# Transformer block in fp32 on one core: the attention's value products taken two chunk steps at a time

## The chip, the cores and the metric

One core of a Trainium2 chip runs the whole kernel. The metric is the device time of one execution in microseconds; lower is better. Its engines are TensorE (PE; PEld is its weight loading), VectorE (DVE), ScalarE (ACT), GpSimd (POOL) and SyncE (SP), which issues the transfers.

## The reference

For 32 sequences of 512 rows and 256 features, in fp32: `x = x + attention(layernorm(x))`, then `x = x + 0.5 * ffn(layernorm(x))`.

The attention is linear: 16 heads of 16 features, `phi(x) = elu(x) + 1` of the projected queries and keys, in 4 chunks of 128 rows, with a state S and a running sum of keys z carried from chunk to chunk:

```python
scores = jnp.where(mask, jnp.einsum('bqd,bkd->bqk', qi, ki), 0)
num = jnp.einsum('bqk,bkd->bqd', scores, vi) + jnp.einsum('bqd,bde->bqe', qi, S)
den = jnp.sum(qi * (jnp.cumsum(ki, axis=1) + z[:, None, :]), axis=-1, keepdims=True)
out = num / den
S2 = S + jnp.einsum('bkd,bke->bde', ki, vi)
```

The result goes through Wo. The FFN has 1024 hidden features, weights in integers with a scale per group of 128 rows, and SiLU between its two products.

## The kernel before, in words

A pass of the loop works on three sequences at once: the attention of sequence i, the FFN of sequence i - 1, and layer norm, projections and features (phi) of sequence i + 1. Each engine has its own instruction list, written out by hand in a function: `pe_iteration`, `ve_iteration`, `ac_iteration`, `po_iteration`, `sp_iteration`. An engine works its list in order; `w.need(event, shift, k)` puts a wait for an event of this or a neighbouring pass in front of the next instruction. Flags A, Fn, N say which of the three parts a pass has. Pass 0 has no FFN, passes 1 to 30 have all, pass 31 has no next sequence, pass 32 only an FFN.

The attention has U = 8 steps: u = 4 t + c, for two halves t of the heads and four chunks c. For a step:
- `scores(u)` (L442): four matmuls into two PSUM banks `sc[0]` and `sc[1]`. It waits until the scores of the step before have left these banks.
- The causal mask: `mask_half` (L601) on VectorE multiplies a bank by `causal` into the tile `probs[u % 2]`. For the steps in `POOL_MASKS` = 2, 3, 4, 5 the second half goes another way: `copy_scores` (L943) on ScalarE copies `sc[1]` to `probs`, GpSimd multiplies it in place (L1005).
- `update_state(u)` (L464) adds the chunk to the state, `snapshot(u)` (L709) on VectorE copies it out, `from_state(u)` (L452) multiplies the queries by it.
- `values(u)` (L480): the masked scores times the values, into `num[t]`, on tiles of 32 columns of the array; sixteen matmul records, of which four run side by side.
- The reciprocals of the denominators: transposed by `spread_reciprocals` (L512) into a bank and copied out by `reciprocals_out` (L936), once for each t. `attention(t)` (L722) multiplies them in.

Between the steps stands the FFN, for slices j = 0 to 7 of the hidden features: `fc1(j)` (L379, L380) writes two banks, a and b. `ffn_scaled(j)` (L850, ScalarE) takes bank a, `ffn_sum(j)` (L687, VectorE) adds bank b, `ffn_silu(j)` (L858, L861, ScalarE) applies SiLU and makes the high part s_hi, and GpSimd the low part s_lo (L998). Behind the steps come the next sequence's `x_transposes` (L347), whose two banks ScalarE copies to xt_hi (L839) and VectorE to xt_lo (L631), then `project_kq(0)` and `project_kq(1)` (L317, twelve matmuls each), and the second FFN product `fc2` and the output projection (also L317).

PSUM has eight banks: num[0], num[1], state_acc, sc[0], sc[1], and a ring of three. `RING` gives each use of a ring bank its number, in order of time; a use waits for the last reader of the use before it in the same bank (`free_bank`). `BORROWED` puts some uses into the other banks.

On TensorE the middle of a pass reads: scores(0), k transposes, fc1(0), fc1(1), update(0), fc1(2), scores(1), update(1), values(0); then for u = 2 to 7: fc1(u + 1), reciprocals at u = 2 and 4, scores(u), update(u), from_state(u - 1), values(u - 1), with x_transposes at u = 6 behind them. project_kq(0), from_state(7), values(7), project_kq(1) follow. On ScalarE, for j = 3 to 6: scale slice j, reciprocals out at 3 and 5, copy the scores of step j - 1, SiLU of slice j - 1; then slice 7 scaled, xt_hi, and SiLU of 6 and 7.

Of the kernel before, what the change touches and what calls it, by code (L numbers as in the profile page):

```python
# [29 lines left out]
P = 128  # L30
# [43 lines left out]
def build(nc, x, wq_t, bq, wk_t, bk, wv_t, bv, wo_t, bo, gamma, beta, q1, sc1, b1, q2, sc2, b2, out):  # L74
# [4 lines left out]
    C = S // P  # L79
# [15 lines left out]
    with ExitStack() as ctx:  # L95
# [66 lines left out]
        def by_group(ap):  # L162
# [11 lines left out]
        RING = {"ht0": 0, "v1": 2, "kt1": 1, "f1a": 0, "f1b": 2, "f2a": 1, "f2b": 0, "f3a": 2, "f3b": 1, "rb0": 0,  # L174
                "f4a": 2, "f4b": 1, "f5a": 0, "f5b": 2, "rb1": 1, "f6a": 0, "f6b": 2, "f7a": 1, "f7b": 0,
                "xt0": 2, "xt1": 1, "k0": 0, "q0": 1, "z0": 0, "wo0": 2, "z1": 1}
        USES = list(RING)
        NEXT_USES = {"xt0", "xt1", "k0", "q0"}

        BORROWED = {"v0": state_acc, "kt0": state_acc, "ht1": num[0], "f0a": num[0], "f0b": num[1], "wo1": num[0]}  # L180
# [51 lines left out]
        def need_masked(w, u, r):  # L232
# [29 lines left out]


        LAST_READ = {
            "ht0": (ht_l, 0), "v1": (v_sb, 3), "kt1": (kt_sb, 1), "rb0": (rb_sb, 0),
            "rb1": (rb_sb, 1), "z0": (e_out, 0), "z1": (e_out, 1), "wo0": (e_x1, 0),
            "xt0": (xt_l, 0), "xt1": (xt_l, 1), "k0": (phi, 0), "q0": (phi, 1),
        } | {f"f{j}{ab}": ((f_a, f_b)["ab".index(ab)], j) for j in range(FT) for ab in "ab"}

# [4 lines left out]
        def free_bank(w, use, present):  # L274

            if use == "v0":
                w.need(snap, -1)
                return
            if use == "kt0":
                w.need(v_sb, 0, 1)  # L280
                return
            if use == "ht1":
                w.need(e_x1, -1, 1)
                return
            if use == "f0a":
                w.need(ht_l, -1, 1)
                return
            if use == "f0b":
                if "rb0" in present:
# [60 lines left out]
        def pe_iteration(e, i, A, Fn, N, N2, preparation=None, bias_products=None, first=False):  # L350
# [95 lines left out]
            def from_state(u):  # L446

                t, c = divmod(u, C)
                if c:
                    n = t * (C - 1) + c - 1  # L450
                    w.need(snap, 0, n)
                    e.matmul(num[t][:, c * P:(c + 1) * P], state[:, n % 3, :], phi_q[:, t, c * P:(c + 1) * P],  # L452
                             start=False, stop=False, skip_group_check=True)

            def update_state(u):
                t, c = divmod(u, C)
# [11 lines left out]
            def values(u):  # L468

                t, c = divmod(u, C)  # L470
                for r in range(2):
                    need_masked(w, u, r)
                w.need(v_sb, 0, c)
                if c == 0 and Fn:
                    w.need(f_b, -1, 0)
                if u == C:
                    w.need(rden, 0)
                for odd in range(2):
                    for pair in range(HT // 2):
                        last = e.matmul(  # L480
                            num[t][32 * pair:32 * pair + 32, c * P:(c + 1) * P],
                            v_pad[:, c, t * HT // 2 + pair, 2 * odd:2 * odd + 2, :],
                            probs[u % 2][:, 2 * pair + odd, :],
                            start=(c == 0 and odd == 0), stop=(odd == 1), skip_group_check=True)
                av_pe.done(last)

            def denominators(shift):
# [12 lines left out]
            def denominators_back(shift):  # L500

                w.need(den_sb, shift)
                for x in range(2):
                    last = e.transpose(num[1][:, (2 + x) * P:(3 + x) * P], den_rows[:, x * P:(x + 1) * P], ident[:, :])
                den_tr.done(last)

            def spread_reciprocals(t):

# [29 lines left out]
                k_transposes(0)  # L538
                k_transposes(1)
            fc1(0)  # L540
            fc1(1)
            if not A and Fn:
                fc1(2)
                for j in range(FT):
                    if j + 3 < FT:
                        fc1(j + 3)
                    fc2_group(j)
                return
            if A:
                update_state(0)  # L550
            fc1(2)
            if A:
                scores(1)
                update_state(1)
                values(0)
            for u in range(2, U):
                if u < 7:
                    fc1(u + 1)
                if A and u in (2, 4):
                    spread_reciprocals(u // 2 - 1)  # L560
                if A:
                    scores(u)
                    update_state(u)
                    from_state(u - 1)
                    values(u - 1)
                if u == 6 and N:
                    x_transposes()
            if preparation:
                preparation()
            project_kq(0)  # L570
            if A:
                from_state(U - 1)
                values(U - 1)
            project_kq(1)
            if bias_products:
                bias_products()
# [12 lines left out]


        def half_probs(u, r):
            return probs[u % 2][:, r * HV:(r + 1) * HV, :]

        def mask_half(e, w, u, r):

            w.need(sc_pe, 0, u)
            if u >= 2:
                w.need(av_pe, 0, u - 2)
            else:
                w.need(av_pe, -1)  # L600
            masked[r].done(e.tensor_tensor(  # L601
# [31 lines left out]
        def ve_iteration(e, i, A, Fn, N, N2, preparation=(None, None, None)):  # L633
# [121 lines left out]
            if Fn and not A:  # L755
                ffn_scaled(0)
            ffn_sum(0)
            ffn_sum(1)
            if A:
                snapshot(0)  # L760
            ffn_sum(2)
            if A:
                mask(1)
                snapshot(1)
            for u in range(2, U):
                if u < 7:
                    ffn_sum(u + 1)
                if A:
                    mask(u)
                    snapshot(u)  # L770
# [4 lines left out]
                if N and u == 6:  # L775
                    for t in range(T):
                        ve_lo(e, w, ring_bank(f"xt{t}")[:, :], xt_hi, xt_lo, t, xt_h, 1, xt_l)
# [56 lines left out]
        def ac_iteration(e, i, A, Fn, N, N2, preparation=None):  # L834
# [81 lines left out]
            if A:  # L916
# [5 lines left out]
                for n in range(2):  # L922
# [4 lines left out]
            ffn_scaled(0)  # L927
            ffn_scaled(1)
            ffn_silu(0)
            ffn_scaled(2)  # L930
            ffn_silu(1)

            def reciprocals_out(t):
                if A:
                    w.need(rb_pe, 0, t)
# [2 lines left out]
            def copy_scores(u):  # L938

                if A and u in POOL_MASKS:  # L940
                    w.need(sc_pe, 0, u)
                    w.need(av_pe, 0, u - 2)
                    copied.done(e.activation(half_probs(u, 1), sc[1][:, :].rearrange("p (h q) -> p h q", h=HV), ACT.Copy))  # L943

            for j in range(3, FT - 1):
                ffn_scaled(j)
                if j in (3, 5):
                    reciprocals_out((j - 3) // 2)
                copy_scores(j - 1)
                ffn_silu(j - 1)  # L950
            copy_scores(FT - 2)
            ffn_scaled(FT - 1)
            if N:
                for t in range(T):
                    w.need(v_pe, 0)
# [349 lines left out]
```

How the kernel before makes its waits and increments, by code:

```python
    def need(self, event, shift=0, k=None):  # L63
        k = event.per - 1 if k is None else k
        if self.known.get((id(event), shift), -1) >= k:
            return
        self.known[(id(event), shift)] = k
        value = event.value(self.i + shift, k)
        if not isinstance(value, int) or value > 0:
            self.engine.wait_ge(event.sem, value)
# [1034 lines left out]
        @block.sync  # L1106
        def _(e):
            e.dma_start(x_in[:, :, :], x_v[0]).then_inc(load.sem, 16)
            src = {"q": wq_t, "k": wk_t, "v": wv_t, "o": wo_t}
            for n in WORDER:
                e.dma_start(stage_of(n), src[n].rearrange("(t p) n -> p t n", p=P)).then_inc(p_wdma[n], 16)
            e.dma_start(bias_o[:, :], on_all(bo)).then_inc(p_dma, 16)
            for t in range(T):
                e.dma_start(w1_i[t], q1[t * P:(t + 1) * P, :]).then_inc(p_wdma["1"], 16)
            early(e, store)
            e.wait_ge(p_const, CONSTS - 1)
            e.wait_ge(p_zero, 1)
            sp_iteration(e, -1, False, False, True, True, lambda: e.wait_ge(p_v, V_W1))
            for n in range(2):
# [10 lines left out]
            with e.Fori(1, B - 2) as i:  # L1131
                sp_iteration(e, i, True, True, True, True)
            sp_iteration(e, B - 2, True, True, True, False)
            sp_iteration(e, B - 1, True, True, False, False)
            sp_iteration(e, B, False, True, False, False)
            e.wait_ge(store.sem, store.value(B - 1, 1))
```

## Time and profile before

| | |
|---|---|
| time, median of 3 runs | 1603.43 us (1603.17 to 1604.33) |
| the profiled execution | 1604.64 us, span 1602.9 us |
| mean granted TensorE clock | 0.990 |
| PE busy | 1556.0 us, 97% |
| DVE busy | 1238.6 us, 77% |
| ACT busy | 1177.6 us, 73% |
| POOL busy | 827.3 us, 52% |

The profile is of one execution. Times inside it count from the first instruction. Busy time of PE is modelled at the ends of matmuls: a row's duration reaches over the start of the next, and the distance between two starts tells how long TensorE was held.

### The profile page before, as it was taken

What the parts mean: (1) busy time and instruction counts of PE and PEld (TensorE: products, weight loads), DVE (VectorE), ACT (ScalarE), POOL (GpSimd) and SP (SyncE); (2) the same over time, 40 slices, a digit from 0 to 9 for tenths busy, and PEclk for the clock granted to TensorE, in tenths of its full rate; (3) what the DMA queues carried; (4) which work ended last, traced back from release to release, by engine and by line L of the source; (5) the groups of instructions that cost most, each with busy time, mean ns of one, the idle gap of its engine ahead of it and who ended that gap; (6) DMA issues with size and microseconds to landing.
All of it is one profiled execution on the core that took longest, in us unless ns stands there. A gap on an engine that the chain in (4) does not pass through costs nothing.

```text
span 1602.9 us, 39179 instructions
## 1 busy us (share of the span) xinstructions
PE 1556.0 (97%) x13668; PEld 1346.5 (84%) x13668; DVE 1238.6 (77%) x2587; ACT 1177.6 (73%) x2045; POOL 827.3 (52%) x594
## 2 busy tenths in 40 slices
PE   5799999999999999999999999999999999999997
PEld 4588888888888888888888888888888888888886
DVE  6777787777787777787778787778787778787865
ACT  4487777787777787777797777787777787777763
POOL 3255445555445555445555445555445555445553
PEclk8799999999999999999999999999999999999999
DMA  7756675545664546764456664446765546764440
GB/s 187 172 125 141 170 159 127 128 123 143 170 164 118 121 134 144 170 168 120 115 132 147 170 154 133 113 130 151 170 145 130 126 124 155 170 158 116 114 99 27
DMA packets 153943, 222.94 MB, mean 139 GB/s; under 512 B 20032, under 2 KB 71488, under 8 KB 153920
## 3 DMA queue, kind: packets, MB, share of 16 engines
q1 hardware_dynamic: 152560, 222.63, 57.5%
q8 instruction: 14, 0.23, 0.1%
q10 hardware_dynamic: 1360, 0.01, 0.0%
q14 instruction: 9, 0.07, 0.0%
HBM read 138.69 MB, written 83.89 MB: 139 GB/s over the span
## 4 chain that ended last, share of the span: by engine, by line
PE 64%; DVE 15%; ACT 9%; issue 9%; DMA 2%; DVEq 1%; SPq 1%; ACTq 0%; POOL 0%
PE ring L317 31%; DVE probs L601 7%; PE sc L317 6%; PE num L480 5%; PE sc L442 4%; PE ring L379 4%; ACT silu_f L850 3%; PE ring L380 3%; PE num L317 3%; PE state_acc L317 3%; ACT silu_f L858 2%; DVE x_hat L623 2%; DVE silu_f L687 2%; PE num L452 2%; DVE xt_lo L631 1%
## 5 line engine op out<-in xcount | busy, mean ns | idle before, releaser
L998 POOL TENSOR_TENSOR s_lo<-silu_f,s_hi 128x512 fp32r<-128x512 f32 x256 | 341.6, 1339 | 357.5 <-ACT s_hi L861 357.4
L687 DVE SCALAR_TENSOR_TENSOR silu_f<-ring,scale,silu_f 128x512 f32<-128x512 f32 x222 | 166.4, 749 | 177.1 <-ACT silu_f L850 176.1
L317 PE MATMUL ring<-w_hi,s_hi 128*128 128x256 f32 x992 | 282.0, 284 | 1.4 <-issue 1.4
L317 PE MATMUL ring<-w_lo,s_hi 128*128 128x256 f32 x992 | 278.9, 281 | 0.0
L317 PE MATMUL ring<-w_hi,s_lo 128*128 128x256 f32 x992 | 278.8, 281 | 0.0
L601 DVE TENSOR_TENSOR probs<-sc,causal 128x512 f32<-128x512 f32 x384 | 251.0, 681 | 12.2 <-PE sc L442 8.8
L1018 POOL TENSOR_TENSOR qk<-qk,phi_q 128x512 f32<-128x512 f32 x64 | 82.8, 1294 | 264.0 <-DVE qk L654 264.0
L442 PE MATMUL sc<-q_stack,k_stack 96*128 96x256 f32 x1024 | 189.0, 300 | 11.7 <-issue 4.8
L317 PEld LDWEIGHTS ring<-w_hi,s_hi 128*128 128x128 f32 x992 | 187.2, 189 | 15.5 <-issue 14.0
L1005 POOL TENSOR_TENSOR probs<-probs,causal 128x512 f32<-128x512 f32 x128 | 165.2, 1291 | 56.9 <-ACT probs L943 51.5
L379 PE MATMUL ring<-gt_hi,w_q 128*128 128x512 f32 x441 | 193.7, 439 | 0.0
L317 PEld LDWEIGHTS ring<-w_lo,s_hi 128*128 128x128 f32 x992 | 187.1, 189 | 1.2
L317 PEld LDWEIGHTS ring<-w_hi,s_lo 128*128 128x128 f32 x992 | 187.4, 189 | 0.0
L442 PEld LDWEIGHTS sc<-q_stack,k_stack 96*128 96x128 f32 x1024 | 153.3, 191 | 37.7 <-DVE probs L601 14.5
L380 PE MATMUL ring<-gt_lo,w_q 128*128 128x512 f32 x441 | 174.3, 395 | 0.0
L858 ACT ACTIVATE silu_f<-silu_f 128x512 f32<-128x512 f32 x256 | 159.8, 624 | 14.7 <-DVE silu_f L687 10.9
L982 ACT ACTIVATE state<-num 128x256 f32<-128x256 f32 x32 | 12.3, 384 | 215.2 <-PE num L495 215.2
L861 ACT ACTIVATE s_hi<-silu_f 128x512 fp32r<-128x512 f32 x256 | 162.0, 633 | 8.1
L850 ACT ACTIVATE silu_f<-ring,bias,scale 128x512 f32<-128x512 f32 x217 | 166.2, 766 | 0.5
L480 PE MATMUL num<-probs,v_pad 128*32 128x128 f32 x4096 | 166.0, 280 | 0.5 <-DVE probs L601 0.3
L480 PEld LDWEIGHTS num<-probs,v_pad 128*32 128x32 f32 x4096 | 96.9, 110 | 31.8 <-issue 1.1
L379 PEld LDWEIGHTS ring<-gt_hi,w_q 128*128 128x128 f32 x441 | 83.0, 188 | 44.9 <-issue 30.7
(188 smaller groups left out, 3972.0 us busy)
## 6 DMA issues: line engine op xcount, KB each, us to landing
k_stack<-k_rows SPq DMA_DIRECT2D x192, 256.0 KB, 4.1
q_stack<-q_rows SPq DMA_DIRECT2D x384, 128.0 KB, 6.1
k_rows<-silu_f SPq DMA_DIRECT2D x128, 256.0 KB, 3.6
q_rows<-probs SPq DMA_DIRECT2D x128, 256.0 KB, 4.7
x_in<-in_x SPq DMA_DIRECT2D x32, 512.0 KB, 8.1
xb<-in_x SPq DMA_DIRECT2D x32, 512.0 KB, 7.8
out<-clip SPq DMA_DIRECT2D x64, 256.0 KB, 7.2
silu_f<-in_q SPq DMA_DIRECT2D x2, 512.0 KB, 9.6
```

The lines of the kernel that those rows point to most:

```text
L317: last = e.matmul(target, a, b, start=(n == 0), stop=(n == 3 * len(pairs) - 1))
L379: e.matmul(bank_[:, :], w1_q[:, t, cols], gt_hi[:, t, :], start=True, stop=False)
L380: f_pe.done(e.matmul(bank_[:, :], w1_q[:, t, cols], gt_lo[:, t, :], start=False, stop=True))
L442: last = e.matmul(sc[r][:, 2 * n * P:2 * (n + 1) * P], k_stack[:, t, pair, toks], q_stack[:, t, pair, :, toks], start=True, stop=True)
L480: last = e.matmul(num[t][32 * pair:32 * pair + 32, c * P:(c + 1) * P], v_pad[:, c, t * HT // 2 + pair, 2 * odd:2 * odd + 2, :], probs[u % ...
L601: masked[r].done(e.tensor_tensor(half_probs(u, r), sc[r][:, :].rearrange("p (h q) -> p h q", h=HV), causal[:, None, :].to_broadcast([P, HV ...
L687: f_b.done(e.scalar_tensor_tensor(out=slot, in0=ffn_bank(j, 1, A)[:, :], scalar=scale_1[:, 1, j:j + 1], in1=slot, op0=ALU.mult, op1=ALU.add))
L850: f_a.done(e.activation(silu_f[:, j % SLOTS, :], ring_bank(f"f{j}a")[:, :], ACT.Identity, bias=bias_1[:, j:j + 1], scale=scale_1[:, 0, j:j ...
L858: silu.done(e.activation(slot, slot, ACT.Silu))
L861: sh.done(e.activation(s_hi[:, j, :], slot, ACT.Copy))
L998: sl.done(e.tensor_tensor(s_lo[:, j, :], silu_f[:, j % SLOTS, :], s_hi[:, j, :].bitcast(F32), ALU.subtract))
L1005: po_masked.done(e.tensor_tensor(half_probs(j, 1), half_probs(j, 1), causal[:, None, :].to_broadcast([P, HV, P]), ALU.mult))
```

## The change

- Values of two steps are taken together: a new `attend(u)` issues from_state(u), from_state(u + 1), values(u), values(u + 1). The loop on TensorE goes by two steps: scores(u), update(u - 1), attend(u - 2), scores(u + 1), update(u), reciprocals at u = 2 and 4, fc1(u + 1), fc1(u + 2). scores(1) and update(0) move ahead of fc1(1). x_transposes stand behind the loop; attend(6) stands between the two projections.
- Since two steps' masked scores wait while a third is made, `probs` gets a third tile, which lies in the memory of phi_k; step u uses `probs[u % 3]`, and the next features into phi_k wait for the values of step 5 at least.
- The product from the state comes first into `num`, so it carries the start flag.
- GpSimd masks the second half at steps 2, 4, 6 instead of 2, 3, 4, 5.
- The reciprocals go back through num[1] (an entry of BORROWED) instead of ring banks; the ring's numbers shift.
- VectorE and ScalarE follow in the new order.

```diff
+        probs.append(phi_k[:, :, :].rearrange("p t s -> p (t s)").rearrange("p (h q) -> p h q", q=P))
...
-                "f4a": 2, "f4b": 1, "f5a": 0, "f5b": 2, "rb1": 1, "f6a": 0, "f6b": 2, "f7a": 1, "f7b": 0,
-                "xt0": 2, "xt1": 1, "k0": 0, "q0": 1, "z0": 0, "wo0": 2, "z1": 1}
+                "f4a": 0, "f4b": 2, "f5a": 1, "f5b": 0, "f6a": 2, "f6b": 1, "f7a": 0, "f7b": 2,
+                "xt0": 1, "xt1": 0, "k0": 2, "q0": 1, "z0": 0, "wo0": 2, "z1": 1}
...
-        POOL_MASKS = (2, 3, 4, 5)
+        POOL_MASKS = (2, 4, 6)
...
+            def attend(u):
+
+                for m in (u, u + 1):
+                    from_state(m)
+                for m in (u, u + 1):
+                    values(m)
...
             if A:
+                scores(1)
                 update_state(0)
+            fc1(1)
             fc1(2)
-            if A:
-                scores(1)
-                update_state(1)
-                values(0)
-            for u in range(2, U):
-                if u < 7:
-                    fc1(u + 1)
-                if A and u in (2, 4):
-                    spread_reciprocals(u // 2 - 1)
+            for u in range(2, U, 2):
                 if A:
                     scores(u)
+                    update_state(u - 1)
+                    attend(u - 2)
+                    scores(u + 1)
                     update_state(u)
-                    from_state(u - 1)
-                    values(u - 1)
-                if u == 6 and N:
-                    x_transposes()
+                    if u <= C:
+                        spread_reciprocals(u // 2 - 1)
+                fc1(u + 1)
+                if u + 2 < FT:
+                    fc1(u + 2)
+            if N:
+                x_transposes()
             if preparation:
                 preparation()
             project_kq(0)
             if A:
-                from_state(U - 1)
-                values(U - 1)
+                attend(U - 2)
             project_kq(1)
...
-                w.need(av_pe, s - 1, m * C + C - 1)
+                w.need(av_pe, s - 1, max(m * C + C - 1, 5))
...
-            for j in range(3, FT - 1):
-                ffn_scaled(j)
-                if j in (3, 5):
-                    reciprocals_out((j - 3) // 2)
-                copy_scores(j - 1)
-                ffn_silu(j - 1)
-            copy_scores(FT - 2)
-            ffn_scaled(FT - 1)
+            for u in range(2, U, 2):
+                copy_scores(u)
+                ffn_scaled(u + 1)
+                if u <= C:
+                    reciprocals_out(u // 2 - 1)
+                ffn_silu(u)
+                if u + 2 < FT:
+                    ffn_scaled(u + 2)
+                    ffn_silu(u + 1)
...
             attention_hi(0)
-            ffn_silu(FT - 2)
             ffn_silu(FT - 1)
```

## Rows read from the trace of the kernel before

**Rows 1.** The page: busy time, share of the span and instructions of each engine.

```profile
PE 1556.0 (97%) x13668; PEld 1346.5 (84%) x13668; DVE 1238.6 (77%) x2587; ACT 1177.6 (73%) x2045; POOL 827.3 (52%) x594
```

**Rows 2.** Windows: stretch, its length, busy per engine, clock, DMA share, GB/s.

```profile
178.10:1526.70 1348.60, 1342.66 (x11930) 1165.04 (x11929) 1062.76 (x2231) 1031.83 (x1793) 716.57 (x504) 1.00 0.59 141
```

**Rows 3.** PE timeline, one line a pass apart: start, us, engine, line, operation.

```profile
804.35 0.38 PE L504 MATMUL num<-ident,state 128*128 128x128 f32 x2
...
852.51 0.38 PE L504 MATMUL num<-ident,state 128*128 128x128 f32 x2
```

**Rows 4.** PE timeline, from scores(0) to step 2.

```profile
808.28 0.64 PE L442 MATMUL sc<-q_stack,k_stack 96*128 96x256 f32 x4
808.76 0.60 PE L422 MATMUL state_acc<-ident,phi_k 128*128 128x128 f32 x4
...
811.66 0.48 PE L379 MATMUL ring<-gt_hi,w_q 128*128 128x512 f32 x1
811.98 0.40 PE L380 MATMUL ring<-gt_lo,w_q 128*128 128x512 f32 x1
812.21 0.40 PE L379 MATMUL ring<-gt_hi,w_q 128*128 128x512 f32 x1
...
813.57 0.65 PE L480 MATMUL num<-probs,v_pad 128*32 128x128 f32 x16
814.14 0.49 PE L379 MATMUL ring<-gt_hi,w_q 128*128 128x512 f32 x1
814.47 0.40 PE L380 MATMUL ring<-gt_lo,w_q 128*128 128x512 f32 x1
...
815.64 1.10 PE L442 MATMUL sc<-q_stack,k_stack 96*128 96x256 f32 x4
816.58 0.38 PE L464 MATMUL state_acc<-v_pad,k_tok 128*128 128x128 f32 x2
```

**Rows 5.** PE timeline, the first eight of sixteen value matmuls of one step.

```profile
827.60 0.43 PE L480 MATMUL num<-probs,v_pad 128*32 128x128 f32 x8
```

**Rows 6.** PE timeline, steps 5 to the second projections.

```profile
827.28 0.39 PE L452 MATMUL num<-phi_q,state 128*128 128x128 f32 x2
827.60 0.64 PE L480 MATMUL num<-probs,v_pad 128*32 128x128 f32 x16
...
830.84 0.50 PE L317 MATMUL ring<-xt_hi,wk_hi 128*128 128x512 f32 x1
...
834.63 0.50 PE L317 MATMUL sc<-xt_hi,wk_hi 128*128 128x512 f32 x1
```

**Rows 7.** ACT timeline, a step of the loop, and the copies of x.

```profile
821.08 0.76 ACT L850 ACTIVATE silu_f<-ring,bias,scale 128x512 f32<-128x512 f32 x1
821.76 0.60 ACT L936 ACTIVATE qk<-ring 128x512 f32<-128x512 f32 x1
822.25 0.59 ACT L943 ACTIVATE probs<-sc 128x512 f32<-128x512 f32 x1
822.73 0.63 ACT L858 ACTIVATE silu_f<-silu_f 128x512 f32<-128x512 f32 x1
...
823.93 0.76 ACT L850 ACTIVATE silu_f<-ring,bias,scale 128x512 f32<-128x512 f32 x1
...
828.87 1.08 ACT L839 ACTIVATE xt_hi<-ring 128x512 fp32r<-128x512 f32 x2 [1.57 <-PE ring L347]
```

**Rows 8.** DVE timeline: both half masks of step 0, and xt_lo.

```profile
810.16 1.28 DVE L601 TENSOR_TENSOR probs<-sc,causal 128x512 f32<-128x512 f32 x2
...
829.49 1.29 DVE L631 TENSOR_TENSOR xt_lo<-ring,xt_hi 128x512 fp32r<-128x512 f32 x2
```

**Rows 9.** Windows around pauses of PE: columns as in rows 2.

```profile
45.80:47.80 2.00, 0.04 (x1) 0.01 (x1) 0.00 (x0) 0.60 (x1) 0.42 (x1) 1.00 1.11 244
...
47.90:51.30 3.40, 3.40 (x26) 2.76 (x27) 0.89 (x2) 0.60 (x1) 1.27 (x1) 0.50 1.07 370
...
1552.60:1555.50 2.90, 1.22 (x26) 0.71 (x19) 2.30 (x4) 0.57 (x2) 2.90 (x3) 1.00 0.00 0
```

More of the change, by code:

```diff
@@ L173, in build @@
         ring = [bank(f"ring{n}") for n in range(3)]
-        RING = {"ht0": 0, "v1": 2, "kt1": 1, "f1a": 0, "f1b": 2, "f2a": 1, "f2b": 0, "f3a": 2, "f3b": 1, "rb0": 0,
-                "f4a": 2, "f4b": 1, "f5a": 0, "f5b": 2, "rb1": 1, "f6a": 0, "f6b": 2, "f7a": 1, "f7b": 0,
-                "xt0": 2, "xt1": 1, "k0": 0, "q0": 1, "z0": 0, "wo0": 2, "z1": 1}
+        RING = {"ht0": 0, "v1": 2, "kt1": 1, "f1a": 0, "f1b": 2, "f2a": 1, "f2b": 0, "f3a": 2, "f3b": 1,
+                "f4a": 0, "f4b": 2, "f5a": 1, "f5b": 0, "f6a": 2, "f6b": 1, "f7a": 0, "f7b": 2,
+                "xt0": 1, "xt1": 0, "k0": 2, "q0": 1, "z0": 0, "wo0": 2, "z1": 1}
         USES = list(RING)
         NEXT_USES = {"xt0", "xt1", "k0", "q0"}
-        BORROWED = {"v0": state_acc, "kt0": state_acc, "ht1": num[0], "f0a": num[0], "f0b": num[1], "wo1": num[0]}
+        BORROWED = {"v0": state_acc, "kt0": state_acc, "ht1": num[0], "rb0": num[1], "rb1": num[1], "f0a": num[0], "f0b": num[1], "wo1": num[0]}
         FFN_USES = {"ht0", "ht1", "z0", "z1"} | {f"f{j}{ab}" for j in range(FT) for ab in "ab"}
@@ L264, in build @@
         LAST_READ = {
-            "ht0": (ht_l, 0), "v1": (v_sb, 3), "kt1": (kt_sb, 1), "rb0": (rb_sb, 0),
-            "rb1": (rb_sb, 1), "z0": (e_out, 0), "z1": (e_out, 1), "wo0": (e_x1, 0),
+            "ht0": (ht_l, 0), "v1": (v_sb, 3), "kt1": (kt_sb, 1),
+            "z0": (e_out, 0), "z1": (e_out, 1), "wo0": (e_x1, 0),
             "xt0": (xt_l, 0), "xt1": (xt_l, 1), "k0": (phi, 0), "q0": (phi, 1),
@@ L287, in free_bank @@
                 return
+            if use == "rb0":
+                w.need(f_b, -1, 0)
+                w.need(rden, 0)
+                return
+            if use == "rb1":
+                w.need(rb_sb, 0, 0)
+                return
             if use == "f0b":
-                if "rb0" in present:
+                if "wo0" in present:
                     w.need(rden, 0)
@@ L450, in from_state @@
                     n = t * (C - 1) + c - 1
+                    if c == 1 and Fn:
+                        w.need(f_b, -1, 0)
+                    if u == C + 1:
+                        w.need(rb_sb, 0, 1)
                     w.need(snap, 0, n)
                     e.matmul(num[t][:, c * P:(c + 1) * P], state[:, n % 3, :], phi_q[:, t, c * P:(c + 1) * P],
-                             start=False, stop=False, skip_group_check=True)
+                             start=(c == 1), stop=False, skip_group_check=True)
             def update_state(u):
@@ L473, in values @@
                 w.need(v_sb, 0, c)
[L474 to L477, printed above, removed]
                 for odd in range(2):
@@ L482, in values @@
                             v_pad[:, c, t * HT // 2 + pair, 2 * odd:2 * odd + 2, :],
-                            probs[u % 2][:, 2 * pair + odd, :],
-                            start=(c == 0 and odd == 0), stop=(odd == 1), skip_group_check=True)
+                            probs[u % 3][:, 2 * pair + odd, :],
+                            start=False, stop=(odd == 1), skip_group_check=True)
                 av_pe.done(last)
@@ L540, in pe_iteration @@
             fc1(0)
-            fc1(1)
             if not A and Fn:
+                fc1(1)
                 fc1(2)
@@ L549, in pe_iteration @@
             if A:
+                scores(1)
                 update_state(0)
+            fc1(1)
             fc1(2)
-            if A:
-                scores(1)
-                update_state(1)
-                values(0)
-            for u in range(2, U):
-                if u < 7:
-                    fc1(u + 1)
-                if A and u in (2, 4):
-                    spread_reciprocals(u // 2 - 1)
+            for u in range(2, U, 2):
                 if A:
                     scores(u)
+                    update_state(u - 1)
+                    attend(u - 2)
+                    scores(u + 1)
                     update_state(u)
-                    from_state(u - 1)
-                    values(u - 1)
-                if u == 6 and N:
-                    x_transposes()
+                    if u <= C:
[5 more added lines that the diff above has]
+                x_transposes()
             if preparation:
@@ L591, in half_probs @@
         def half_probs(u, r):
-            return probs[u % 2][:, r * HV:(r + 1) * HV, :]
+            return probs[u % 3][:, r * HV:(r + 1) * HV, :]
         def mask_half(e, w, u, r):
             w.need(sc_pe, 0, u)
-            if u >= 2:
-                w.need(av_pe, 0, u - 2)
+            if u >= 3:
+                w.need(av_pe, 0, u - 3)
             else:
@@ L757, in ve_iteration @@
             ffn_sum(0)
[L758 to L761, printed above, removed]
             if A:
                 mask(1)
-                snapshot(1)
+                snapshot(0)
+            ffn_sum(1)
             for u in range(2, U):
-                if u < 7:
-                    ffn_sum(u + 1)
                 if A:
                     mask(u)
-                    snapshot(u)
+                    snapshot(u - 1)
                     if u == 5:
@@ L774, in ve_iteration @@
                             preparation[2]()
-                if N and u == 6:
-                    for t in range(T):
-                        ve_lo(e, w, ring_bank(f"xt{t}")[:, :], xt_hi, xt_lo, t, xt_h, 1, xt_l)
+                ffn_sum(u)
+            if N:
+                for t in range(T):
+                    ve_lo(e, w, ring_bank(f"xt{t}")[:, :], xt_hi, xt_lo, t, xt_h, 1, xt_l)
             if A:
@@ L926, in ac_iteration @@
                                             ring_bank(f"kt{n}")[:, :].rearrange("p (c d) -> p c d", c=2), ACT.Copy))
[L927 to L931, printed above, removed]
             def reciprocals_out(t):
@@ L941, in copy_scores @@
                     w.need(sc_pe, 0, u)
-                    w.need(av_pe, 0, u - 2)
+                    w.need(av_pe, *((0, u - 3) if u >= 3 else (-1,)))
                     copied.done(e.activation(half_probs(u, 1), sc[1][:, :].rearrange("p (h q) -> p h q", h=HV), ACT.Copy))
-            for j in range(3, FT - 1):
-                ffn_scaled(j)
-                if j in (3, 5):
-                    reciprocals_out((j - 3) // 2)
-                copy_scores(j - 1)
-                ffn_silu(j - 1)
-            copy_scores(FT - 2)
-            ffn_scaled(FT - 1)
+            ffn_scaled(0)
+            ffn_scaled(1)
+            ffn_silu(0)
+            ffn_scaled(2)
+            ffn_silu(1)
+            for u in range(2, U, 2):
[7 more added lines that the diff above has]
+                    ffn_silu(u + 1)
             if N:
```

## The prediction

> **What bounds the kernel now.** I read the page first: TensorE is busy for 97% of the span [rows 1]. Busy there is modelled, so I took the stretch of 28 equal passes next: TensorE is busy in 1342.7 of 1348.6 us, and ScalarE in 1031.8 [rows 2]. The two rows of one line of the code a pass apart [rows 3] give the period: 852.51 - 804.35 = 48.16 us. Each us added to the chain through TensorE in a pass therefore costs 30 us (passes 1 to 30 hold attention, FFN and the next projections). TensorE's timeline then shows what the totals hide: starts of matmuls tell pauses that busy time doesn't. In [rows 4] the scores of step 2 take 816.58 - 815.64 = 0.94 us, where those of step 0 take 808.76 - 808.28 = 0.48: they wait for masks. Before the first projections there is about 0.2 more, until xt_lo is there. Such waits come to some 0.7 us a pass. ScalarE's timeline [rows 7] is the second thing to see: through the steps it works nearly without a gap, and strictly in the order written. So the middle of the pass has two engines near their limit, TensorE and ScalarE, and what one hands to the other late is paid.
>
> **What the change saves.** The values are 16 matmul records on tiles of 32 columns. From their first start to the next matmul's take 0.57 us (813.57 to 814.14 [rows 4]). Eight of them take 0.43 us, all sixteen 0.64 [rows 5, 6], so a round of four costs 0.11 and four rounds 0.44; the leftover is 0.13. Into the values the step is 827.60 - 827.28 = 0.32 for two passes of 0.11, 0.10 too much. The second matmul behind them starts 0.33 after the first (814.14, 814.47), where a steady step is 0.23 (811.98, 812.21): 0.10. A switch in and out thus costs 0.10 + 0.13 + 0.10 = 0.33 us. Two steps together make 4 groups of 8: 4 x 0.33 = 1.3 us a pass saved. A double group lasts 0.57 + 4 x 0.11 = 1.01 us, and its two products from the state 0.44.
>
> **What moves without a price.** The third tile of scores, in phi_k: its last readers of this batch, the k transposes, stand before step 2 on TensorE, and the next batch's features wait for step 5's values, long done: nothing. Reciprocals through num[1]: they leave the ring and wait for ones long done. GpSimd loses a mask (not the bound), ScalarE a copy of 0.49 us, and VectorE gains one half mask of 0.6 us, at steps 3 and 5 instead of sharing them: it has 2.3 us from scores(3) to scores(4), and needs 1.2. If that cover went, it would cost the 0.6.
>
> **What it costs: the order of ScalarE against TensorE.** I keep the clock of [rows 4], scores(0) at 808.28, and put the new order on it with durations of the rows. Hand-overs: VectorE or ScalarE to TensorE 0.06 (xt_lo in [rows 8] ends at 830.78, the projections it holds in [rows 6] start at 830.84), TensorE to ScalarE an estimated 0.04 behind a matmul of 0.40. Scores that start after a wait take 0.23 + 0.11 for their second pair.
> - scores(1) now stands right behind fc1(0). mask(0) ends at 811.44 [rows 8]: the second pair starts at 811.50, the next instruction at 811.84. update(0) and the first matmul of fc1(1) follow: the second, which ends bank a, starts 0.14 + 0.32 later (as 811.66 to 811.98), 812.29. ScalarE scales slice 1 at 812.73.
> - ScalarE then does, in order: scale 0.67, SiLU and its copy 1.19 (822.73 to 823.93), scale, SiLU and copy: 3.7 us. Only now copy_scores(2): 816.43 to 817.02. scores(3), which TensorE reaches at about 816.4 (scores(2) 814.08, update, attend(0) with 0.22 + 0.10 + 1.01), holds until 817.08: a wait of 0.7.
> - 0.34 for the second pair, update(2) 0.22, reciprocals 0.36, fc1(3)'s bank a 0.32 + 0.40 + 0.04: ScalarE scales slice 3 at 818.75. It had stood idle for 1.8 us since the copy. The cycle is closed: copy_scores(4) comes only behind scale(3), reciprocals, SiLU(2), scale(4), SiLU(3) = 0.67 + 0.49 + 1.19 + 0.67 + 1.19 = 4.2, so at 822.94 to 823.54; scores(5), reached at 822.4, waits until 823.60 (1.2); scale(5) starts at 825.27. Two steps last 825.27 - 818.75 = 6.5 us. Before, values(0) to values(5) are 827.60 - 813.57 = 14.03 us [rows 4, 6], 5.6 for two steps, with an fc1 ahead of each score to cover the copy.
> - Again for steps 6 and 7: copy_scores(6) ends at 830.06, scores(7) waits 1.2 and is done at 830.46, scale(7) starts at 831.35.
> - The transposes of x stand behind fc1(7) and nothing is left between them and the projections, where one step and its values lay before. TensorE is through with them at 832.60. ScalarE does SiLU(6) first (832.01 to 833.20), then the two copies of [rows 7] at 828.87 (1.08 us), VectorE the last half of the pair at 829.49 in [rows 8]: end 835.10, projections at 835.16 instead of 830.84. A pause of 2.56 us.
> - The first projections take 2.90 (twelve of 0.24), then the double group 0.44 + 0.10 + 1.01: the second projections start at 839.61, before at 834.63 [rows 6]. This is 4.98 us later. Behind that point TensorE has no wait in the trace before, and ScalarE and VectorE reach it earlier relative to TensorE than they did: nothing is added, and nothing is there to be given back.
>
> So 30 x 4.98 = 149.4 us. The last attention pass has no projections to wait for, but its FFN product then waits for the last SiLU and s_lo behind the same late scale(7): 3.3 more, estimated. The first has no FFN, and weights keep it waiting: 1, estimated. Sum 153.7.
>
> **The clock.** A pause of 1.96 us of TensorE (45.80 to 47.80) is followed by a granted clock of 0.50, 1.2 GHz, for the 3.4 us after; 1.68 us of pause in 1552.60 to 1555.50 leaves it at 1.00 [rows 9]. The new pause of 2.56 is longer than the one that lost it, with dense work on both sides. Such a spell takes half of 3.4 us, so 1.7; part lies in the pause: 1.6. Bounds: 0 and 30 x 1.6 = 48 us. Neither row is of this place, so I take the middle, 24. The Trainium skill (TensorE: Matmul & The Clock Gate, section HAM oscillation) has pauses of DMA waits, longer than this one, bring the clock down, and calls shorter ones safe; by that the 24 would be 0. The row at 47.90 speaks against it.
>
> Sum: the profiled execution took 1604.6 us (span 1602.9 and 1.7 around it); 1604.6 + 153.7 + 24 = 1782.3. The median of the runs shown is 1.2 lower: **1781 us**.
>
> **Rivals.**
> - A, the waits as above and the clock stays: 1757 us. For it: the idle pause in 1552.60 to 1555.50.
> - B, the clock falls in each pass: 1805. For it: a pass 1.6 us longer may meet the same state each time.
> - C, the copies and fc1 overlap better than I have it and only the pause before the projections is new: 2.56 - 0.2 - 1.3 = 1.1 us a pass, 1636. Against it: ScalarE has shown no instruction out of order.
> - D, on the other side: the values' switches are what TensorE pays, and ScalarE, rid of a copy, keeps up: 31 x 1.3 = 40 us less, 1563. It decides only where copy_scores(4) ends before 822.4; it has 4.8 us of work ahead on ScalarE, and would have to do it in 3.6, and the transposes would have to find cover besides.
> - E, gain and waits cancel (1.3 us of waits): 1603.
>
> **How the numbers follow.** Forecast (clock lost in some passes) 0.38, A 0.24, B 0.24, C 0.07, D 0.05, E 0.02. Forecast, A and B differ by the clock alone, and their waits may be 0.4 us a pass off (12 us): 1742 to 1815 holds some 0.84. This measurement can tell about 0.2% from no change. Faster 0.05, same 0.02, slower 0.93.
>
> **What would show it.** In the new trace: ScalarE waiting some 1.8 us for the first half of fc1(3), (5), (7); scores(5) and (7) with 1.2 us inside; a pause of 2.5 us between the transposes of x and the projections; four groups of 32 value records of about 1.0 us a pass; a period of 53.1 us, or up to 54.7 with the clock below 1. Wrong if the copies of the scores of steps 4 and 6 start as soon as these scores are there, or if TensorE stays at 97%.

## The result

| | median | runs | ratio to before, 95% interval |
|---|---|---|---|
| before | 1603.88 us | 1603.17 to 1604.85 | |
| changed | 1804.89 us | 1803.14 to 1805.92 | 1.1252 [1.1232, 1.1271] |

The change costs 201 us, 12.5%. The forecast was 1781 us with a range of 1742 to 1815; rival B, the same waits with the clock lost in each pass, gave 1805.

The page of the changed kernel, its line of busy times. It answers to [rows 1].

```profile
PE 1614.3 (90%) x13668; PEld 1379.3 (76%) x13668; DVE 1271.5 (71%) x2619; ACT 1166.9 (65%) x2013; POOL 774.1 (43%) x562
```

TensorE issues the same 13668 matmuls and falls from 97% to 90%. Its busy time grew by 58 us, though no work was added: some matmuls became slower. The windows (columns as in [rows 2]) show where. The first is the stretch of equal passes, the next two are the start of the first projections in two passes that follow each other, and the last is the same place in pass 1.

```profile
178.10:1723.10 1545.00, 1410.82 (x12059) 1207.51 (x12058) 1103.95 (x2292) 1028.84 (x1775) 674.02 (x479) 0.97 0.50 126
934.70:938.10 3.40, 3.37 (x8) 2.69 (x9) 1.14 (x1) 2.54 (x5) 3.07 (x3) 0.50 0.00 0
989.30:992.70 3.40, 3.33 (x8) 2.65 (x9) 1.18 (x2) 2.54 (x5) 3.07 (x3) 0.50 0.00 0
...
116.40:119.80 3.40, 3.32 (x16) 2.77 (x16) 1.18 (x2) 3.31 (x6) 3.07 (x3) 1.00 0.00 0
```

The clock is at 0.50, 1.2 GHz, for 3.4 us at the same place of each pass. The clock records have such a spell in every pass from 2 to 30, each 54.61 us behind the last; before, there was none in this stretch. In pass 1 the clock stays at 1.00 at this place. In the run e4 below, where the clock stays up in all equal passes, TensorE is busy for 1568.5 us, so some 46 of the 58 us are the clock's.

TensorE's timeline of one pass. The two rows of L512 (L504 in [rows 3]) are a pass apart.

```profile
903.93 0.38 PE L512 MATMUL num<-ident,state 128*128 128x128 f32 x2
...
907.88 0.64 PE L450 MATMUL sc<-q_stack,k_stack 96*128 96x256 f32 x4
...
910.50 1.10 PE L450 MATMUL sc<-q_stack,k_stack 96*128 96x256 f32 x4 [0.16 <-DVE probs L615]
...
915.76 0.50 PE L450 MATMUL sc<-q_stack,k_stack 96*128 96x256 f32 x2
916.68 0.50 PE L450 MATMUL sc<-q_stack,k_stack 96*128 96x256 f32 x2 [0.41 <-ACT phi_k L947]
...
921.78 0.50 PE L450 MATMUL sc<-q_stack,k_stack 96*128 96x256 f32 x2
923.18 0.50 PE L450 MATMUL sc<-q_stack,k_stack 96*128 96x256 f32 x2 [0.90 <-ACT probs L947]
...
931.17 1.23 PE L355 MATMUL ring<-ident,x_hat 128*128 128x128 f32 x8
934.73 0.79 PE L325 MATMUL ring<-xt_hi,wk_hi 128*128 128x512 f32 x1 [2.33 <-DVE xt_lo L645]
935.32 0.63 PE L325 MATMUL ring<-xt_lo,wk_hi 128*128 128x512 f32 x1
935.75 0.63 PE L325 MATMUL ring<-xt_hi,wk_lo 128*128 128x512 f32 x1
...
940.69 0.50 PE L325 MATMUL sc<-xt_hi,wk_hi 128*128 128x512 f32 x1
...
958.57 0.38 PE L512 MATMUL num<-ident,state 128*128 128x128 f32 x2
```

The period is 958.57 - 903.93 = 54.64 us, 6.5 over the one before. The scores of steps 3 and 5 fall apart into two pairs; the second waits for ScalarE's copy (L947). Behind the transposes of x TensorE pauses for 2.33 us, and the projections then start 0.43 apart (935.32, 935.75) instead of 0.23. The same pause stands in pass 1, where it cost no clock:

```profile
116.48 0.50 PE L325 MATMUL ring<-xt_hi,wk_hi 128*128 128x512 f32 x1 [2.33 <-DVE xt_lo L645]
```

ScalarE's timeline of the same steps shows the other end of the waits; it answers to [rows 7].

```profile
912.33 0.78 ACT L860 ACTIVATE silu_f<-ring,bias,scale 128x512 f32<-128x512 f32 x1 [1.49 <-PE ring L388]
...
914.86 0.62 ACT L868 ACTIVATE silu_f<-silu_f 128x512 f32<-128x512 f32 x1
915.51 0.63 ACT L871 ACTIVATE s_hi<-silu_f 128x512 fp32r<-128x512 f32 x1
916.05 0.58 ACT L947 ACTIVATE phi_k<-sc 128x512 f32<-128x512 f32 x1
918.35 0.78 ACT L860 ACTIVATE silu_f<-ring,bias,scale 128x512 f32<-128x512 f32 x1 [1.72 <-PE ring L388]
...
922.55 0.58 ACT L947 ACTIVATE probs<-sc 128x512 f32<-128x512 f32 x1
924.85 0.78 ACT L860 ACTIVATE silu_f<-ring,bias,scale 128x512 f32<-128x512 f32 x1 [1.72 <-PE ring L388]
...
932.78 1.07 ACT L849 ACTIVATE xt_hi<-ring 128x512 fp32r<-128x512 f32 x2
```

Each engine waits for the other once in two steps. ScalarE copies the scores of step 4 only behind two SiLUs (922.55), TensorE stands 0.90 us until then, and ScalarE stands 1.72 us until TensorE has come from there to fc1(5). 918.35 to 924.85 is 6.50 us for two steps. The waits list of the equal passes says the same in totals (waiting engine and line, the releaser, us, times, longest).

```profile
ACT silu_f L860 <- PE ring L388: 174.4, 112, 1.7
...
PE ring L325 <- DVE xt_lo L645: 65.3, 28, 2.3
PE sc L450 <- ACT probs L947: 50.3, 56, 0.9
PE sc L450 <- ACT phi_k L947: 11.6, 28, 0.4
```

### The profile page after: what moved, and what is told of

Read it like the earlier page. It is cut to its first block, busy times and chain, and to the rows that moved or that the text cites. A ratio compares the mean times of both kernels' runs of the same rounds, so it can differ in the third digit from the quotient of the medians.

```text
span 1803.2 us, 39197 instructions
## 1 busy us (share of the span) xinstructions
PE 1614.3 (90%) x13668; PEld 1379.3 (76%) x13668; DVE 1271.5 (71%) x2619; ACT 1166.9 (65%) x2013; POOL 774.1 (43%) x562
## 4 chain that ended last, share of the span: by engine, by line
PE 55%; ACT 23%; issue 11%; DVE 6%; DMA 2%; SPq 1%; ACTq 1%; DVEq 0%; POOL 0%
PE ring L325 31%; ACT silu_f L860 8%; ACT silu_f L868 7%; PE sc L325 5%; PE sc L450 4%; PE num L325 2%; PE state_acc L325 2%; DVE probs L615 2%; ACT probs L947 2%; DVE x_hat L637 2%; PE ring L388 2%; PE num L488 2%; PE ring L387 2%; ACT qk L940 2%; PE state_acc L476 2%
## 5 line engine op out<-in xcount | busy, mean ns | idle before, releaser
L1007 POOL TENSOR_TENSOR s_lo<-silu_f,s_hi 128x512 fp32r<-128x512 f32 x256 | 330.2, 1290 | 535.0 <-ACT s_hi L871 535.0
L615 DVE TENSOR_TENSOR probs<-sc,causal 128x512 f32<-128x512 f32 x320 | 208.9, 686 | 119.0 <-PE sc L450 114.9
L450 PE MATMUL sc<-q_stack,k_stack 96*128 96x256 f32 x1024 | 212.9, 311 | 86.4 <-ACT probs L947 55.7
L488 PE MATMUL num<-probs,v_pad 128*32 128x128 f32 x3072 | 110.5, 277 | 0.0
L325 PE MATMUL ring<-xt_hi,wk_hi 128*128 128x512 f32 x64 | 42.2, 660 | 73.4 <-DVE xt_lo L645 73.4
L615 DVE TENSOR_TENSOR phi_k<-sc,causal 128x512 f32<-128x512 f32 x96 | 63.4, 688 | 58.3 <-PE sc L450 58.3
```

What stands on the lines that cost most here:

```text
L325: last = e.matmul(target, a, b, start=(n == 0), stop=(n == 3 * len(pairs) - 1))
L450: last = e.matmul(sc[r][:, 2 * n * P:2 * (n + 1) * P], k_stack[:, t, pair, toks], q_stack[:, t, pair, :, toks], start=True, stop=True)
L488: last = e.matmul(num[t][32 * pair:32 * pair + 32, c * P:(c + 1) * P], v_pad[:, c, t * HT // 2 + pair, 2 * odd:2 * odd + 2, :], probs[u % ...
L615: masked[r].done(e.tensor_tensor(half_probs(u, r), sc[r][:, :].rearrange("p (h q) -> p h q", h=HV), causal[:, None, :].to_broadcast([P, HV ...
L1007: sl.done(e.tensor_tensor(s_lo[:, j, :], silu_f[:, j % SLOTS, :], s_hi[:, j, :].bitcast(F32), ALU.subtract))
```

## The experiments

The runs e1 to e5 are each the changed kernel with one edit. m1 is built on the changed kernel, m2, m3 and m4 on m1, m5 on m3, m6 on m5. Each ratio is to runs of the kernel before that were taken beside them, with medians of 1604.5 to 1605.7 us.

**e1, the pause filled with matmuls.**

```diff
+            if N and Fn and A:
+                free_bank(w, "k0", present)
+                for m in range(12):
+                    e.matmul(ring_bank("k0")[:, 0:D], w_hi["q"][:, 0, 0:P], w_hi["k"][:, m % T, :], start=True, stop=True)
             project_kq(0)
```

> The changed kernel with 12 extra matmuls (128x256, of weights, into the bank that the first projections then overwrite) in the pause ahead of the first projections; they add work that isn't used. Theory: the first projections run at 1.2 GHz because of the pause, so with the pause filled the clock stays at 1.00, the first projections take 2.9 us instead of 4.4, and the time falls by 29 x 1.5 = 44 us to 1761 us, the period to 53.1 us. Rival: the slow projections have another cause, or the pause's length isn't what matters: 1805 us, unchanged.

Measured: 1761.45 us, ratio 1.0978 [1.0956, 1.1000]. The timeline and a window over the first projections:

```profile
858.07 1.68 PE L588 MATMUL ring<-wk_hi,wq_hi 128*128 128x256 f32 x12 [0.21 <-DVE silu_f L705]
860.19 0.50 PE L325 MATMUL ring<-xt_hi,wk_hi 128*128 128x512 f32 x1 [0.43 <-DVE xt_lo L649]
...
860.20:863.10 2.90, 2.90 (x13) 2.36 (x14) 1.12 (x1) 2.83 (x5) 2.60 (x3) 1.00 0.00 0
```

The projections still wait for xt_lo and start as long behind scores(0) as in the changed kernel, but the clock is at 1.00, and the period is 53.13 us. So the 1804.9 - 1761.5 = 43.4 us are what the clock took.

**e5, the pause filled with transposes.** This run was made last, on a point that e1 left: what holds the clock. The diff is against e1.

```diff
-                for m in range(12):
-                    e.matmul(ring_bank("k0")[:, 0:D], w_hi["q"][:, 0, 0:P], w_hi["k"][:, m % T, :], start=True, stop=True)
+                for m in range(13):
+                    e.transpose(ring_bank("k0")[:, 0:P], ident[:, :], ident[:, :])
```

> As e1, but the pause is filled with 13 transposes of the identity (128x128, about 0.11 us each, 1.4 us in all) instead of 12 matmuls. The transposes of x ahead of the pause take 1.2 us more, so that between fc1(7) and the projections TensorE has nothing but transposes and pauses for 3.6 us. Theory that the idle time of TensorE alone decides: the clock stays up as in e1, 1761 us. Rival (transposes don't hold the clock as matmuls do, which the Trainium skill states in TensorE: Matmul & The Clock Gate, Part 4, PE-mode transpose): the clock still falls in most passes, 1790 to 1805 us.

Measured: 1761.25 us, ratio 1.0972 [1.0953, 1.0990], the same as e1. The period is 53.13 us. TensorE's timeline and the window of its first projections:

```profile
855.14 1.23 PE L355 MATMUL ring<-ident,x_hat 128*128 128x128 f32 x8
856.59 1.64 PE L588 MATMUL ring<-ident 128*128 128x128 f32 x13 [0.22 <-DVE silu_f L705]
858.70 0.49 PE L325 MATMUL ring<-xt_hi,wk_hi 128*128 128x512 f32 x1 [0.48 <-DVE xt_lo L649]
...
858.70:862.10 3.40, 3.40 (x16) 2.77 (x16) 1.12 (x1) 3.31 (x6) 3.08 (x3) 1.00 0.00 0
```

Here fp32 transposes keep the clock up as matmuls do, which is not what the Trainium skill states in the place that the expectation names. Whether transposes alone would raise a clock that is down, no run shows. The run also closes another reading of the changed kernel: if transposes counted as a pause, TensorE would pause there from 931.17 to 934.73, 3.56 us, with the transposes of x taken in. In e5 the stretch from 855.14 to 858.70 holds nothing but transposes and pauses, 3.56 us as well, and the clock stays at 1.00. So the loss goes with the time without any work.

**e2, attend(6) ahead of both projections.**

```diff
-            project_kq(0)
             if A:
                 attend(U - 2)
+            project_kq(0)
             project_kq(1)
```

> The changed kernel with attend(6) ahead of both projections instead of between them. Theory: it lies in the pause, which shrinks from 2.3 us to about 0.8; the projections start where they did, the clock stays up: 1.55 + 1.5 = 3.05 us a pass, 1805 - 92 = 1713 us. Rival, the clock is lost all the same: 1805 - 47 = 1758 us. Rival, the values move but the projections are late by as much: 1805 us.

Measured: 1711.62 us, ratio 1.0663 [1.0645, 1.0680], 1.4 us from the expectation. TensorE's timeline at the first projections:

```profile
838.01 0.51 PE L325 MATMUL ring<-xt_hi,wk_hi 128*128 128x512 f32 x1 [0.88 <-DVE xt_lo L645]
```

The pause is down to 0.88 us, the matmul takes 0.51 instead of 0.79. Work that does not need xt_lo fills the pause, and saves the clock besides.

**e3, the copies of the scores one SiLU earlier.**

```diff
             ffn_scaled(2)
+            copy_scores(2)
             ffn_silu(1)
             for u in range(2, U, 2):
-                copy_scores(u)
                 ffn_scaled(u + 1)
...
                     ffn_scaled(u + 2)
+                    copy_scores(u + 2)
                     ffn_silu(u + 1)
```

> The changed kernel with ScalarE's copies of the scores each one SiLU earlier: copy_scores(2) ahead of ffn_silu(1), (4) ahead of ffn_silu(3), (6) ahead of ffn_silu(5). Theory (the place of the copies in ScalarE's list is what the scores wait for): the waits of 0.7 + 1.2 + 1.2 us inside scores(3), (5), (7) vanish, 3.0 us a pass: 1805 - 90 = 1715 us with the clock still lost in each pass, 1670 if the lower period frees it. Rival (ScalarE is simply short of time in the steps, and the SiLUs that are put off hold the next slices instead): under 1 us a pass, 1775 or more.

Measured: 1704.14 us, ratio 1.0623 [1.0601, 1.0645]: 101 us less than the changed kernel. TensorE's timeline, scores(5) and the first projections:

```profile
821.77 0.73 PE L450 MATMUL sc<-q_stack,k_stack 96*128 96x256 f32 x4
...
832.39 0.78 PE L325 MATMUL ring<-xt_hi,wk_hi 128*128 128x512 f32 x1 [2.33 <-DVE xt_lo L645]
...
935.55 0.50 PE L325 MATMUL ring<-xt_hi,wk_hi 128*128 128x512 f32 x1 [2.33 <-DVE xt_lo L645]
```

The four scores run in one piece, no engine does less work, and so the place of the copies in the list was the cause of the waits. The time lies between the two expectations: the pause stays at 2.33 us in every pass, but the clock falls in 21 of the 29 passes from 2 to 30 and stays up in the other 8 (832.39 against 935.55). Periods are 51.4 to 51.7 us with the spell and 50.1 without.

**e4, SiLU(6) behind the copies of x.**

```diff
-                ffn_silu(u)
                 if u + 2 < FT:
+                    ffn_silu(u)
...
             attention_hi(0)
+            ffn_silu(FT - 2)
             ffn_silu(FT - 1)
```

> The changed kernel with ScalarE's SiLU of slice 6 put off behind the copies of x to xt_hi, as it was before the change. Theory: the projections start 0.9 us earlier (then held by the second transposes), the pause is 1.4 us: 1805 - 27 = 1778 us with the clock lost, 1733 us if a pause of 1.4 us leaves it up. Rival (the pause hangs on VectorE's mask(7), snapshot and ffn_sum(7) and not on ScalarE): 1805 us.

Measured: 1733.37 us, ratio 1.0801 [1.0783, 1.0819]. TensorE's timeline at the first projections, and the window of the pause:

```profile
845.32 0.51 PE L325 MATMUL ring<-xt_hi,wk_hi 128*128 128x512 f32 x1 [1.41 <-DVE xt_lo L645]
...
843.90:845.30 1.40, 0.01 (x1) 0.00 (x0) 1.40 (x4) 1.37 (x4) 1.40 (x1) 1.00 0.00 0
```

A pause of 1.41 us leaves the clock up. 0.9 us of pause less saved 2.4 us a pass.

**m1, three mends together** (e2, e3 and e4 in one kernel).

> The changed kernel with three mends together: ScalarE's copies of the scores one SiLU earlier, attend(6) ahead of both projections, and SiLU(6) behind the copies to xt_hi. Theory (the merge of the values does save its switches, and only the orders lost it): waits of 3.0 us, late projections of 0.9, attend(6) of 1.55 in the pause and the clock's 1.5 go: 54.6 - 7.0 = 47.6 us a pass, 0.6 under the kernel before, about 1588 us. Rival (the merge saves nothing, the waits were all): the four switches of 0.33 are still there, 48.9 us a pass, 1625 us.

Measured: 1610.86 us, ratio 1.0040 [1.0026, 1.0054]: between theory and rival, 23 us over the one and 14 under the other, so that the time alone doesn't decide between them. The waits for ScalarE's copies and for xt_lo are gone (one of 0.2 us in scores(1), for VectorE's mask, stays), but the list of waits of its equal passes has a new one:

```profile
PE num L488 <- POOL probs L1016: 17.0, 28, 0.6
```

attend(6), moved up, now reaches GpSimd's mask of step 6 before it is done. That is 0.6 us a pass, the excess of the period (48.20 us) over the theory's 47.6; the expectation had not looked at GpSimd.

**m2, m1 with the values taken apart again.** It alone tells what the merge is worth, since few waits hide it here.

```diff
-                for m in (u, u + 1):
+                second = (u + 1) % C
+                for m in (u, u + 1) if second == 1 else (u,):
                     from_state(m)
-                for m in (u, u + 1):
-                    values(m)
+                values(u)
+                if second == 1:
+                    update_state(u + 1)
+                else:
+                    from_state(u + 1)
+                values(u + 1)
...
-                    update_state(u - 1)
                     attend(u - 2)
```

> m1 with an instruction of full width between the values of every two steps (update(1), from_state(3), update(5), from_state(7) moved between them), so that the array is switched eight times a pass instead of four; no work is added. Theory: 4 x 0.33 = 1.3 us a pass more than m1, 1588 + 40 = 1628 us; where a pair lies before a wait, a part of it is hidden: 1610 or more. Rival (a switch costs nothing by itself): as m1.

Measured: 1648.14 us, ratio 1.0271 [1.0255, 1.0287], 37.3 us over m1; the period goes from 48.20 to 49.38 us, 1.18 for four switches, 0.30 each. One step on TensorE's timeline of m1, then the same step in m2:

```profile
767.20 0.63 PE L450 MATMUL sc<-q_stack,k_stack 96*128 96x256 f32 x4
769.22 0.74 PE L450 MATMUL sc<-q_stack,k_stack 96*128 96x256 f32 x4
...
784.94 0.65 PE L450 MATMUL sc<-q_stack,k_stack 96*128 96x256 f32 x4
...
785.74 0.64 PE L488 MATMUL num<-probs,v_pad 128*32 128x128 f32 x16
786.32 0.49 PE L476 MATMUL state_acc<-v_pad,k_tok 128*128 128x128 f32 x2
786.73 0.65 PE L488 MATMUL num<-probs,v_pad 128*32 128x128 f32 x16
787.31 0.74 PE L450 MATMUL sc<-q_stack,k_stack 96*128 96x256 f32 x4
```

The two matmuls of update(1), which are all that stands between the two groups of values, hold TensorE for 786.73 - 786.32 = 0.41 us, where they take 0.22 elsewhere. From scores(2) to scores(3) it is 2.02 us in m1 and 2.37 in m2, and the next two steps grow by as much: 0.34 a switch. The fourth, in attend(6), costs only 0.2, since it lies partly in the wait for GpSimd.

**m3, m1 with scores(1) and update(0) behind fc1(1).**

```diff
             fc1(0)
+            if A:
+                fc1(1)
...
                 scores(1)
                 update_state(0)
-            fc1(1)
             fc1(2)
```

> m1 with scores(1) and update(0) behind fc1(1) instead of ahead of it. Theory: the wait for the mask of step 0 in scores(1), 0.65 us, lies behind fc1(1) then: 20 us less than m1, about 1568 us. Rival (ScalarE and VectorE take the time again in step 2): as m1.

Measured: 1589.09 us, ratio 0.9903 [0.9888, 0.9918]: 21.8 us under m1, as much as the theory had between them, and a little faster than the kernel before. The period is 47.47 us, 0.73 less.

**m4, m1 with `POOL_MASKS = (6,)`.**

> m1 with the masks of steps 2 and 4 on VectorE alone (POOL_MASKS = (6,)), so without two of ScalarE's copies and two of GpSimd's masks. Theory: ScalarE gains 1.0 us a pass, VectorE is given 1.2; neither is the bound with the mends made: within 10 us of m1. Rival (ScalarE's total work still bounds the steps): 15 us or more under m1. Rival (VectorE becomes late with the second halves, and scores(3) and (5) wait for it): 15 us or more over m1.

Measured: 1613.88 us, ratio 1.0059 [1.0044, 1.0074], 3 us from m1, with the same period of 48.20 us. Which engine masks steps 2 and 4 makes no difference once the order is right.

**m5, m3 with GpSimd's masks ahead of the s_lo before them.**

```diff
             ffn_lo(0)
-            ffn_lo(1)
-            for j in range(2, FT):
+            for j in range(2, FT + 1):
                 if A and j in POOL_MASKS:
...
+                ffn_lo(j - 1)
                 if A and j == FT - 2:
...
-                ffn_lo(j)
```

> m3 with each of GpSimd's masks ahead of the s_lo of the slice before instead of behind it. In the profile of m3 the values of step 6 wait 0.7 us for GpSimd's mask of step 6, which starts 2.5 us after its copy is there, behind an s_lo that waits for ScalarE. Theory: the mask ends 1.2 us earlier, the wait goes, 0.7 us a pass: 1589 - 20 = 1569 us. Rival (the projections behind are held by xt_lo just as long): as m3, 1589 us.

Measured: 1578.66 us, ratio 0.9837 [0.9823, 0.9850]. GpSimd's timeline of m3, the mask of step 6 behind the s_lo of slice 5:

```profile
771.23 1.29 POOL L1010 TENSOR_TENSOR s_lo<-silu_f,s_hi 128x512 fp32r<-128x512 f32 x1 [1.06 <-ACT s_hi L872]
772.47 1.28 POOL L1017 TENSOR_TENSOR probs<-probs,causal 128x512 f32<-128x512 f32 x1
```

and of m5, mask first, the only wait of TensorE that the list has for m5's equal passes, and the transposes that it stands in:

```profile
766.04 1.31 POOL L1016 TENSOR_TENSOR probs<-probs,causal 128x512 f32<-128x512 f32 x1
767.29 1.30 POOL L1010 TENSOR_TENSOR s_lo<-silu_f,s_hi 128x512 fp32r<-128x512 f32 x1
...
PE ring L355 <- ACT x_hat L917: 1.5, 9, 0.2
...
745.23 0.92 PE L355 MATMUL ring<-ident,x_hat 128*128 128x128 f32 x4
745.99 0.60 PE L355 MATMUL num<-ident,x_hat 128*128 128x128 f32 x4
```

The wait for GpSimd is gone, but half of it came back elsewhere (10 us gained of 20). The list puts the new wait at 1.5 us in all, but starts show it in every pass: the first four transposes ahead of the FFN hold TensorE for 745.99 - 745.23 = 0.76 us, where they take 0.44 in m3, since ScalarE's last copy to x_hat is late. On average this is 0.36 us a pass. The projections start 0.03 us later behind the values than in m3.

**m6, m5 with the reciprocals' transposes between fc1(3) and fc1(4), and fc1(5) and fc1(6).**

```diff
-                    if u <= C:
-                        spread_reciprocals(u // 2 - 1)
                 fc1(u + 1)
+                if A and u <= C:
+                    spread_reciprocals(u // 2 - 1)
```

> m5 with the transposes of the reciprocals between fc1(3) and fc1(4), and between fc1(5) and fc1(6), instead of ahead of both. Theory: they cover the 0.2 us that bank b of fc1(4) and of fc1(6) waits for ScalarE's scaling (a bank used by the slice before): 0.4 us a pass, 12 us under m5. Rival (ScalarE then waits for the reciprocals and passes the time on): as m5 or over.

Measured: 1567.02 us, ratio 0.9766 [0.9749, 0.9782]. The window of its equal passes:

```profile
178.10:1486.00 1307.90, 1304.57 (x11929) 1160.12 (x11928) 1086.75 (x2262) 1031.97 (x1765) 675.78 (x476) 1.00 0.61 146
```

The period is 46.71 us, 0.42 less than m5's, as the theory had it. m6 beats both kernels, by 37 and by 238 us.

## Why the prediction was right, and where it was off

**The chain of waits.** Taken from the start of scores(0), the forecast and the trace after (907.88) are:

| | forecast | measured |
|---|---|---|
| scale of slice 1 | 4.45 | 912.33: 4.45 |
| copy of scores 2 | 8.15 | 916.05: 8.17 |
| scale of slice 3 | 10.47 | 918.35: 10.47 |
| copy of scores 4 | 14.66 | 922.55: 14.67 |
| scale of slice 5 | 16.99 | 924.85: 16.97 |
| copies of x | 24.92 | 932.78: 24.90 |
| first projections | 26.88 | 934.73: 26.85 |
| second projections | 31.33 | 940.69: 32.81 |

Up to the first projections each step holds to 0.03 us. The sum rests on two things: that an engine does its list in order, and that the durations of the rows stay. Both held. e3 shows that this mechanism, and not ScalarE's total work, made the waits, and e4 and e2 that the pause had the causes named. ScalarE's wait, 1.8 us in the forecast for slices 3, 5 and 7, is 1.72 for two of them and 1.29 for slice 7; the forecast's own times give these (818.75 - 817.02 = 1.73 and 831.35 - 830.06 = 1.29), and the 1.8 was a slip. The wait inside scores(5), 1.2 us in the forecast, shows as 0.90 of idle time, since busy time runs to the modelled end of the matmul before; by starts the second pair comes 923.18 - 921.78 = 1.40 us after the first, and 0.22 of that is its share without a wait: 1.18.

**The step that was mis-sized: the clock.** The forecast put the loss at 24 us, the middle of 0 and 48. Measured by e1 it is 43.4 us: 29 passes times 1.5 (54.64 - 53.13 = 1.51). The price of one spell, 1.6, was near; the share of passes was wrong. It was not one half but all from pass 2 on, which was rival B, with a chance of 0.24. The 24 was the middle of two cases and described neither, so that 1781 came within 24 us of the time owes something to luck. The forecast's case of some passes spared came only in e3. Why all passes lose the clock at 54.6 us, 21 of 29 at 50 to 52 us, and pass 1 does not, though the pause is 2.33 us each time, stays open. Rival B's reason, that a pass of this length meets the same state again, fits the spells at 54.61 us from each other, but no run tests it. The Trainium skill's rule on pauses (TensorE: Matmul & The Clock Gate, section HAM oscillation), by which the 24 would be 0, does not hold here, though the section also tells of a kernel whose clock swung with short pauses: the windows at 934.70 and 989.30 show that 2.33 us of pause can be enough. A reading of the forecast was loose besides: the 1.68 us of pause in 1552.60 to 1555.50 are two pauses, of 1.45 and about 0.26 us, so that row said less for rival A than it seemed.

**The ends.** The kernel with the clock kept, e1, takes 1761 us, rival A had 1757. Of the 4 us, 1.6 are in the kernel before, which took 1605.0 us beside e1 and 1603.4 in the forecast. The others are in the passes whose prices were estimates: in e1 pass 0 lasts 49.3 instead of 46.8 us (estimated +1), pass 1 56.7 instead of 50.9 (+5.0), and what follows pass 30 takes 80.1 us instead of 76.2 (+3.3).

**The saving.** 0.33 us a switch was read from starts of matmuls; m2 measures 0.34 where no wait lies beside it and 0.30 on average. In m1 the merge is worth 1.2 us of 48 a pass. In the changed kernel it stands against under 5 us of waits and 1.5 of clock, and what it is worth there no run measures. Rival D, that it would decide, needed ScalarE's copies to be in time. With the three mends of m1 they are, but m1 is still 6 us over the kernel before; only m3, m5 and m6, with further mends of the order, are under it. No run makes such mends in the kernel before, which has some 0.7 us of waits a pass, so m6's gain of 37 us isn't shown to be the merge's.

**What cost nothing.** The third tile of scores, the reciprocals through another bank, and the other steps for GpSimd: m4 confirms the last. The first two were not undone by themselves; m6 is faster with both in it, so they cost it no more than it gains. Shifting the ring's numbers while two fc1 stand together did cost a little that the forecast doesn't have: bank b of the second fc1 waits for the scaling of the first, about 0.2 us each time, and m6 wins 12 us by covering two of these waits.

## What to carry to other kernels

When work is regrouped on the busiest engine, put every other engine's list beside the new order and follow one period through by starts and durations: a copy that stands behind two unrelated SiLUs costs its wait on both engines, and no busy share shows it before. Look at what a moved block used to cover: values that stood between the transposes and the projections were worth more as cover than the switches that they cost. When the last wait is mended, read the list of waits again, since the next one (here GpSimd's mask, then x_hat) has been hidden behind it.

## What was not expected of the hardware

A pause of 2.33 us of TensorE, between dense work, was followed by 3.4 us at 1.2 GHz in all 29 passes of 54.6 us and in 21 of 29 passes of 50 to 52 us; in pass 1 of the changed kernel and in the 8 others it wasn't, so the length of the pause alone does not decide. Pauses of 1.41 and 0.88 us (e4, e2) were never followed by it in the equal passes. There 0.9 us of idle time decided over another 1.5. Twelve matmuls or thirteen transposes in the pause, whose output nobody reads, gave some 43 us back.
